# Bias tables of an attention layer: a stage of their own, or made in the first stage and copied in memory beside two feed-forward blocks

## The chip, the cores and the metric

The kernel runs on one core of a Trainium2 chip. The metric is the device time of one execution in microseconds (us). The core has a matrix engine (TensorE, PE in the profile), three engines for elementwise work (VectorE or DVE, ScalarE or ACT, GpSimd or POOL) and SyncE (SP), which issues transfers. Each engine runs its own instructions in order, and they meet at semaphores. Transfers run on 16 shared DMA engines.

## The reference

Eight blocks follow each other, each with a residual sum and a layer norm, on x of 4 x 1024 x 256 in f32: causal attention, two layers of local attention with a gated feed-forward each, attention with a relative position bias, a quantised projection, a state-space block, experts, a linear recurrence, and two more local layers. The change concerns the bias of the fourth block only (16 heads, no mask, 32 buckets):

```
line[h, r] = 4 * rel_emb[bucket(r - 1023), h]      # r = 0..2047
bias[h, q, k] = line[h, k - q + 1023]
out = softmax((Q K^T + bias) / 4) V                # /4 is applied inside the exponential
```

So all that a head needs is one line of 2048 numbers; each query row reads it one step further to the left.

## The kernel before

The program is a chain of some 30 stages. A stage opens its buffers and semaphores, runs a block with one instruction stream for each engine, and ends with a barrier of all engines; nothing of the next stage starts before it. Stages pass their data through DRAM.

`stage_enter` (lines 295 to 371) is the first. SP's queue copies the input in DRAM into the padded array `rows` (4 transfers of 1 MB, L315), writes 24 small strips of zeros (L319, L320), and then loads 32 tiles of the input (`enter_xin`, L326). PE turns each, ACT moves it out of PSUM and stores it as `cols` (L359). Beside them DVE and ACT make the tables of the recurrence (`RecurrenceTables`: DVE, then two sines on ACT after the first 8 tiles, then DVE).

`stage_gated_ffn` runs four times; B0ffn and B1ffn are the two in the layers ahead of the bias attention. GpSimd makes an identity and clears a small tile (L1760), and has nothing else to do in the stage. SP loads weights (`w1` at L1748) and activation rows (L1732, L188), PE does the products (L1834, L1853), ACT the gelu and the stores of the results.

`stage_bias_tables` stands after B1ffn and ahead of Cqkv, the first stage of the bias attention. PE multiplies the embedding by a one-hot table (L1443), DVE scales it by 4 (L1464), SP stores the 16 lines (L1421), waits, and loads two of their columns (`bias_sides`, L1424), from which GpSimd and DVE make the far constants `ext_s` (stored at L1434). Then a loop over 16 heads makes two tables each. SP loads 128 shifted copies of the line (L1431: row p begins p elements later), PE turns the order of the rows round with a flipped identity (L1452) and does the same along the columns for a narrow table (L1457), DVE and ACT move both out of PSUM, and ACT's queue stores `skewed` (960 KB a head) and `near_s` (192 KB a head). Catt reads all three.

```
src = line[bass.ds(it * 2 + s, 1), :]
sp.dma_start(rows[:, s, :], bass.AP(src.tensor, src.offset, [[1, P], [1, W]])).then_inc(rows_in[s], 16)
```

Of the kernel before, what the change touches and what calls it, by code (L numbers as in the profile page):

```python
# [16 lines left out]
ALU = mybir.AluOpType  # L17
# [8 lines left out]
P = 128  # L26
# [268 lines left out]
def stage_enter(nc, x, act0, acts, tables, logs):  # L295

    with ExitStack() as ctx:
        pl = Pool_(nc, ctx, "enter")
        tables.working(pl)
        xin = pl.sb("xin", [P, IN, C])  # L300
# [11 lines left out]
        def _(sp):  # L312
            tables.load(sp, logs)
            for b in range(B):
                sp.dma_start(act0["rows"][b * TP + PAD:(b + 1) * TP, :], x[b * T:(b + 1) * T, :]).then_inc(copied, 16)  # L315
            sp.wait_ge(zeroed, 1)
# [5 lines left out]
            with sp.Fori(0, B) as it:  # L322
                for u in range(NT):
                    sp.wait_ge(t_done, it * NT + (u + 1))
                    apart(sp, pl.sp_unread)
                    sp.dma_start(xin[:, u % IN, :], x[bass.ds(it * T + u * P, P), :]).then_inc(x_in[u % IN], 16)  # L326
            sp.wait_ge(pads, 16 * 2 * B * len(acts))
            sp.wait_ge(copied, 16 * B)

        @block.gpsimd  # L330
        def _(g):
            g.memset(zero[:], 0.0).then_inc(zeroed, 1)
            make_identity(nc, g, ident, made)

        @block.tensor
# [33 lines left out]
        @block.vector  # L369
        def _(v):  # L370
            tables.make(v)

# [555 lines left out]
def stage_thin_attention(nc, name, q_s, k_s, v_s, nm_s, r_s, oT_s, scale, bias=None):  # L928
# [5 lines left out]

    causal = bias is None
# [437 lines left out]
def stage_bias_tables(nc, rel_emb, onehot, line, skewed, near_s, ext_s):  # L1373

    nb, H = rel_emb.shape
    W = 2 * T - P
    cuts = [(c, min(c + 512, W)) for c in range(0, W, 512)]  # L1380
    NC, RING = len(cuts), 5
    with ExitStack() as ctx:
        pl = Pool_(nc, ctx, "bias")
        emb, hot, out = pl.sb("emb", [nb, H]), pl.sb("hot", [nb, 2 * T]), pl.sb("out", [H, 2 * T])
        flip = pl.sb("flip", [P, P])
        rows, win = pl.sb("rows", [P, 2, W]), pl.sb("win", [P, 2, W])
        near = pl.sb("near", [P, 2, 3 * P])
        far, rest, sides = pl.sb("far", [P, 2, NT]), pl.sb("far_rest", [P, NT]), pl.sb("sides", [P, 2])
        far_b = pl.sb("far_b", [P, PARTS, NT], BF16)
        ext = pl.sb("ext", [P, PARTS, NT, P], BF16)  # L1390
        ps = pl.ps("ps", (P, 2 * T))
        nr_ps = [pl.ps(f"near{i}") for i in range(2)]
        loaded, made, flipped, copied, stored = (pl.sem(n) for n in ("loaded", "made", "flipped", "copied", "stored"))
        rows_in = [pl.sem(f"rows_in{i}") for i in range(2)]
        turned, near_turned, win_done, near_done = (pl.sem(n) for n in ("turned", "near_turned", "win_done", "near_done"))
        sides_in, placed, ext_done, ext_out = (pl.sem(n) for n in ("sides_in", "placed", "ext_done", "ext_out"))
        win_out = [pl.sem(f"win_out{i}") for i in range(2)]
        block = ctx.enter_context(nc.Block())

        @block.gpsimd  # L1400
        def _(g):
            g.memset(flip[:], 0.0)
            g.drain()
            g.affine_select(out=flip[:], in_=flip[:], compare_op=ALU.not_equal, fill=1.0, base=-(P - 1),
                            pattern=[[1, P]], channel_multiplier=1).then_inc(flipped, 1)
            g.wait_ge(sides_in, 32)
            for i in range(2):
                g.tensor_copy(far[:, i, :], sides[:, i:i + 1].to_broadcast([P, NT]))
                g.drain()
            g.affine_select(out=far[:, 0, :], in_=far[:, 0, :], compare_op=ALU.is_ge, fill=0.0, base=-2 * H,  # L1410
                            pattern=[[-H, NT]], channel_multiplier=1)
            g.drain()
            g.affine_select(out=far[:, 1, :], in_=far[:, 1, :], compare_op=ALU.is_ge, fill=0.0, base=-H - 1,
                            pattern=[[H, NT]], channel_multiplier=-1).then_inc(placed, 1)

        @block.sync
        def _(sp):
            sp.dma_start(emb[:], rel_emb).then_inc(loaded, 16)
            sp.dma_start(hot[:], onehot).then_inc(loaded, 16)
            sp.wait_ge(copied, 1)  # L1420
            sp.dma_start(line, out[:]).then_inc(stored, 16)  # L1421
            sp.wait_ge(stored, 16)
            for i, col in enumerate((0, 2 * T - 1)):
                sp.dma_start(sides[:, i:i + 1], line[:, col:col + 1].unsqueeze(0).to_broadcast([NT, H, 1]),  # L1424
                             allow_slow_non_contiguous=True).then_inc(sides_in, 16)
            with sp.Fori(0, H // 2) as it:
                for s in range(2):
                    sp.wait_ge(near_turned, it * 2 + (s + 1))
                    apart(sp, pl.sp_unread)
                    src = line[bass.ds(it * 2 + s, 1), :]  # L1430
                    sp.dma_start(rows[:, s, :], bass.AP(src.tensor, src.offset, [[1, P], [1, W]])).then_inc(rows_in[s], 16)  # L1431
            sp.wait_ge(ext_done, 1)
            for k in range(PARTS):
                sp.dma_start(ext_s.rearrange("(h k u) c -> k u h c", k=PARTS, u=NT)[k],  # L1434
                             ext[:, k].rearrange("p u c -> p (u c)")).then_inc(ext_out, 16)
            sp.wait_ge(ext_out, 16 * PARTS)

        @block.tensor
        def _(t):
            t.sem_inc(near_turned, 2)  # L1440
            t.wait_ge(loaded, 32)
            for c in range(0, 2 * T, 512):
                ins = t.matmul(ps[0:H, c:c + 512], emb[:], hot[:, c:c + 512], start=True, stop=True)  # L1443
            ins.then_inc(made, 1)
            t.wait_ge(flipped, 1)
            t.wait_ge(copied, 1)
            with t.Fori(0, H // 2) as it:
                for s in range(2):
                    t.wait_ge(rows_in[s], it * 16 + 16)
                    t.wait_ge(win_done, it * 2 + (s + 1))  # L1450
                    for c, e in cuts:
                        ins = t.matmul(ps[:, c:e], flip[:], rows[:, s, c:e], start=True, stop=True)  # L1452
                    ins.then_inc(turned, 1)
                    t.wait_ge(near_done, it * 2 + (s + 1))
                    for k in range(3):
                        x = T - k * P
                        ins = t.matmul(nr_ps[s][:, k * P:(k + 1) * P], rows[:, s, x:x + P], flip[:], start=True, stop=True)  # L1457
                    ins.then_inc(near_turned, 1)
# [1629 lines left out]
```

## Time and profile before

| | |
|---|---|
| median of 3 runs | 7667.36 us (7658.31 to 7671.06) |
| the profiled execution | 7661.74 us, its span 7660.0 us |
| busy over the span | PE 84%, DVE 61%, ACT 36%, POOL 17% |
| mean granted TensorE clock | 0.92 |
| DMA queues, share of 16 engines | SP's 23.8%, ACT's 13.2%; POOL's none |

Busy shares are means over stages that differ. Since stages are separated by barriers, the span is the sum of the stages, and the length of a stage is read between the first instruction of it on SP's queue and that of the next.

### The profile page before, as it was taken

The numbers are of one execution on the slowest core, as the hardware profiler recorded it, in microseconds if no ns is written. First come the engines' busy times: TensorE is split into PE (matmuls) and PEld (weight loads), VectorE is DVE, ScalarE is ACT, GpSimd is POOL, SyncE is SP. The second block draws the span as 40 slices with busy tenths as digits, with TensorE's granted clock in tenths as the row PEclk, the third lists the DMA queues.
The fourth block names the chain that finished last, engine by engine and source line by source line (L and its number), as shares of the span: only waits on it lengthen the run. The fifth ranks groups of instructions, "written<-read, shape, count | busy, mean of one in ns | idle before, by whom it ended". The sixth has DMA issues, their size and how long they took to land. (4 is left out here: it accounts for less than half of the span.)

```text
span 7660.0 us, 115272 instructions
## 1 busy us (share of the span) xinstructions
PE 6397.9 (84%) x31876; PEld 3356.0 (44%) x31876; DVE 4648.5 (61%) x11517; ACT 2779.5 (36%) x6066; POOL 1304.2 (17%) x1035
## 2 busy tenths in 40 slices
PE   6788868989998966999994387986996888998979
PEld 2333334655555533333332253334554455544655
DVE  5665467733864634888875747984335765347735
ACT  0255514712462200566661104541110255224711
POOL 1101115100610003000000003550002441015100
PEclk9899979989999987999997599997998899999999
DMA  5423244542455255332323221115222355324541
GB/s 177 117 67 70 54 148 153 175 143 73 138 184 169 76 213 188 81 80 71 85 57 106 80 80 56 37 32 143 67 64 74 126 163 183 99 87 151 178 150 54
DMA packets 931136, 851.29 MB, mean 111 GB/s; under 512 B 222216, under 2 KB 785376, under 8 KB 930464
## 3 DMA queue, kind: packets, MB, share of 16 engines
q1 hardware_dynamic: 500624, 522.99, 23.8%
q10 hardware_dynamic: 430080, 323.08, 13.2%
q8 instruction: 206, 3.38, 0.2%
q14 instruction: 226, 1.85, 0.1%
HBM read 503.10 MB, written 346.00 MB: 111 GB/s over the span
## 5 line engine op out<-in xcount | busy, mean ns | idle before, releaser
L1267 ACT ACTIVATE Catt_E<-Catt_t 128x512 f32<-128x512 f32 x1024 | 582.5, 596 | 345.8 <-DVE Catt_t L1230 164.0
L1216 DVE CUSTOM_DVE_ANT_0 Catt_S<-Catt_s,Catt_win 128x1024 f32<-128x1024 f32 x512 | 622.7, 1218 | 90.7 <-PE Catt_s L1139 62.1
L1216 DVE CUSTOM_DVE_ANT_0 Aatt_S<-Aatt_s,Aatt_win 128x128 f32<-128x128 f32 (+7 forms) x512 | 375.6, 757 | 251.4 <-PE Aatt_s L1139 239.8
L1267 ACT ACTIVATE Aatt_E<-Aatt_t 128x512 f32<-128x512 f32 (+3 forms) x768 | 355.2, 489 | 250.2 <-PE Aatt_t L1171 171.5
L1168 PE MATMUL Catt_t<-Catt_Q,Catt_K 123*128 123x512 bf16 x1024 | 369.3, 385 | 38.4 <-ACT Catt_E L1267 17.4
L1139 PE MATMUL Catt_s<-Catt_K,Catt_Q 96*128 96x512 bf16 x1024 | 321.2, 397 | 22.2 <-DMA Catt_K<-k_parts 12.1
L1194 PE MATMUL Catt_o<-Catt_E,Catt_V 128*32 128x256 f32 x4096 | 326.5, 391 | 0.0
L2358 PE MATMUL scan_cum<-scan_X,scan_upto 128*128 128x512 f32 x512 | 265.3, 608 | 25.3 <-DVE scan_X L2427 23.9
L1168 PE MATMUL Aatt_t<-Aatt_Q,Aatt_K 99*128 99x512 bf16 (+3 forms) x768 | 241.4, 333 | 51.9 <-ACT Aatt_E L1267 27.6
L2356 PE MATMUL scan_cum<-scan_X,scan_after 128*128 128x512 f32 x448 | 239.7, 617 | 44.0 <-DVE scan_pi L2438 44.0
L1230 DVE TENSOR_TENSOR Catt_t<-Catt_t,Catt_near 128x384 f32<-128x384 f32 (+1 forms) x384 | 200.4, 522 | 116.6 <-PE Catt_t L1168 112.9
L1139 PE MATMUL Aatt_s<-Aatt_K,Aatt_Q 96*128 96x512 bf16 (+3 forms) x768 | 219.8, 342 | 34.3 <-DVE Aatt_nmax L1216 20.8
L1194 PE MATMUL Aatt_o<-Aatt_E,Aatt_V 128*32 128x256 f32 (+1 forms) x2816 | 218.1, 354 | 0.0
L1168 PEld LDWEIGHTS Catt_t<-Catt_Q,Catt_K 123*128 123x128 bf16 x1024 | 96.4, 97 | 277.2 <-ACT Catt_E L1267 222.0
L2625 ACT ACTIVATE moe_sg<-moe_g 128x512 f32<-128x512 f32 x80 | 47.8, 597 | 367.3 <-PE moe_u L2568 367.2
L2568 PE MATMUL moe_g<-moe_xc,moe_wg 128*128 128x512 f32 x320 | 160.4, 625 | 13.0 <-DVE moe_hid L2701 12.7
L2358 PEld LDWEIGHTS scan_cum<-scan_X,scan_upto 128*128 128x128 f32 x512 | 99.5, 196 | 155.0 <-issue 152.0
L1139 PEld LDWEIGHTS Catt_s<-Catt_K,Catt_Q 96*128 96x128 bf16 x1024 | 59.0, 98 | 243.7 <-DVE Catt_nmax L1216 138.9
L2339 POOL TENSOR_TENSOR scan_pr<-scan_pr,scan_pi 128x1024 f32<-128x1024 f32 x64 | 150.9, 2357 | 42.0 <-DVE scan_pr L2438 42.0
L2356 PEld LDWEIGHTS scan_cum<-scan_X,scan_after 128*128 128x128 f32 x448 | 83.3, 195 | 169.8 <-issue 153.7
L2144 PE MATMUL state_in_z<-state_in_wj,state_in_xc 128*128 128x288 f32 x512 | 142.6, 435 | 16.3 <-DVE state_in_wj L2169 16.3
L2332 POOL TENSOR_TENSOR scan_X<-scan_cs,scan_r 128x1024 f32<-128x1024 f32 x64 | 121.8, 1902 | 192.1 <-DVE scan_X L2427 192.1
(723 smaller groups left out, 14584.6 us busy)
## 6 DMA issues: line engine op xcount, KB each, us to landing
moe_cb<-c_s SPq DMA_DIRECT2D x16, 1024.0 KB
bias_rows<-line SPq DMA_DIRECT2D x16, 960.0 KB, 7.1
skewed<-bias_win ACTq DMA_DIRECT2D x16, 960.0 KB
Catt_win<-skewed SPq DMA_DIRECT2D x16, 960.0 KB, 5.0
rec<-state_in_r ACTq DMA_DIRECT2D x32, 416.0 KB
scan_r<-rec SPq DMA_DIRECT2D x64, 208.0 KB, 2.5
Aatt_Q<-q_parts SPq DMA_DIRECT2D x32, 384.0 KB, 4.4
Aatt_K<-k_parts SPq DMA_DIRECT2D x32, 384.0 KB, 5.6
```

The lines of the kernel that those rows point to most:

```text
L1139: ins = t.matmul(s_ps[j % 2][:, c:d], Q[0:K0, b, h, u * P:(u + 1) * P], K[0:K0, b, h, c:d], start=True, stop=True)
L1168: ins = t.matmul(t_ps[n % 2][:, 0:hi - lo], K[:, b, h, kb * P:(kb + 1) * P], Q[:, b, h, lo:hi], start=True, stop=not diagonal and n not in ...
L1194: ins = t.matmul(o_ps[f:f + 2 * hd, o + k0 * P:o + k1 * P], V[:, b, kb, h, :], blocks[:, h, x, k0:k1, :], start=kb == 0 and c == 0, stop=c ...
L1216: v.tensor_tensor_reduce(out=S[:, j % 2, 0:w], in0=s_ps[j % 2][:, 0:w], in1=win[:, 0 if causal else h, w0:w0 + w], scale=-1.0, scalar=BIG, ...
L1230: v.tensor_tensor(x, x, near[:, b, h, a - (kb - 1) * P:z - (kb - 1) * P], ALU.add).then_inc(near_done, 1)
L1267: a.activation(E[:, kb % NB, h, lo:hi], t_ps[n % 2][:, 0:hi - lo], ACT.Exp, scale=scale).then_inc(exped, 1)
L2144: t.matmul(z_ps[s][:], xc[:, c, kt, q * P + j + 1:q * P + j + 1 + P], wj[:, kt, j, :], start=j == 0 and kt == 0, stop=j == TAPS - 1 and kt ...
L2332: g.tensor_tensor(X[:, m % 4, 0, :].rearrange("p (k e) -> p k e", k=16), cs[:, m % 2, :].rearrange("p (k e) -> p k e", k=16), r[:, m % R, ...
L2339: g.tensor_tensor(pr[:, m % 2, :], pr[:, m % 2, :], pi[:, m % 2, :], ALU.add).then_inc(sum_done, 1)
L2356: t.matmul(cum[i][:, c:c + 512], after[:], X[:, (j - 1) % 4, i, c:c + 512], start=False, stop=False, skip_group_check=True)
L2358: ins = t.matmul(cum[i][:, c:c + 512], upto[:], X[:, j % 4, i, c:c + 512], start=u == 0, stop=True, skip_group_check=True)
L2568: ins = t.matmul(ps[k % 2][:], w[:, kt, j * P:(j + 1) * P], xc[:, c, kt, :], start=kt == 0, stop=kt == KT - 1)
```

## The change

The stage goes. A class `BiasTables` takes its parts:

- In `stage_enter`, SP loads the embedding and the one-hot table ahead of the four copies, and after these waits for the lines, stores them, waits for the store and loads the two columns, all ahead of the zero strips and the tile loop. PE makes the lines; it also turns the middle 512 columns of the lines (four transposes, four products with the flipped identity), so that a second short array `back` holds them in reverse order. DVE copies each result out ahead of the recurrence tables, and makes the far constants behind them. SP stores `back` and the far constants after its loop and waits for them.
- In B0ffn and B1ffn, GpSimd's queue issues for four pairs of heads each one copy from DRAM to DRAM for `skewed` and one for `near_s`: 256 rows of 7680 bytes and 256 of 1536 bytes, each row read one element further left than the one before. GpSimd then waits for all 8 before it can reach the barrier.

```diff
+    def store_lines(self, sp):
+        sp.wait_ge(self.copied, 1)
+        sp.dma_start(self.lines, self.out[:]).then_inc(self.stored, 16)
+        sp.wait_ge(self.stored, 16)
+        for i, col in enumerate((0, 2 * T - 1)):
+            sp.dma_start(self.sides[:, i:i + 1], self.lines[0:self.H, col:col + 1].unsqueeze(0).to_broadcast([NT, self.H, 1]),
+                         allow_slow_non_contiguous=True).then_inc(self.sides_in, 16)
...
+    def copy(self, v):
+        H = self.H
+        v.wait_ge(self.lined, 1)
+        v.tensor_scalar(self.out[:], self.ps[0:H, :], 4.0, None, ALU.mult).then_inc(self.copied, 1)
+        v.wait_ge(self.parts, 1)
+        v.tensor_copy(self.turned[:], self.ps[:, 0:4 * H].rearrange("p (k h) -> p k h", k=4)).then_inc(self.parts_copied, 1)
+        v.wait_ge(self.turned_back, 1)
+        v.tensor_copy(self.back_sb[:], self.ps[0:H, 512:512 + 4 * P]).then_inc(self.back_copied, 1)
...
+    def store(self, sp):
+        sp.wait_ge(self.back_copied, 1)
+        sp.dma_start(self.back, self.back_sb[:]).then_inc(self.ext_out, 16)
+        sp.wait_ge(self.ext_done, 1)
+        for k in range(PARTS):
+            sp.dma_start(self.ext_s.rearrange("(h k u) c -> k u h c", k=PARTS, u=NT)[k],
+                         self.ext[:, k].rearrange("p u c -> p (u c)")).then_inc(self.ext_out, 16)
+        sp.wait_ge(self.ext_out, 16 + 16 * PARTS)
+
+    def spread(self, g, pairs, out):
+
+        for i in pairs:
+            up, down = self.lines[i * 2:i * 2 + 2, P - 1:2 * T], self.back[i * 2:i * 2 + 2, P:4 * P]
+            for src, to, step, w in ((up, self.windows, 2 * T, 2 * T - P), (down, self.nears, 4 * P, 3 * P)):
+                g.dma_start(to.rearrange("(h p) c -> h p c", p=P)[i * 2:i * 2 + 2], bass.AP(src.tensor, src.offset, [[step, 2], [-1, P], [1, w]])
+                            ).then_inc(out, 16)
+        g.wait_ge(out, 32 * len(pairs))
...
             tables.load(sp, logs)
+            bias.load(sp)
             for b in range(B):
                 sp.dma_start(act0["rows"][b * TP + PAD:(b + 1) * TP, :], x[b * T:(b + 1) * T, :]).then_inc(copied, 16)
+            bias.store_lines(sp)
             sp.wait_ge(zeroed, 1)
...
+            bias.store(sp)
             sp.wait_ge(pads, 16 * 2 * B * len(acts))
...
             t.sem_inc(t_done, IN)
+            bias.product(t)
             t.wait_ge(made, 1)
+            bias.turn(t, ident)
...
         def _(v):
+            bias.copy(v)
             tables.make(v)
+            bias.split(v)
...
-def stage_bias_tables(nc, rel_emb, onehot, line, skewed, near_s, ext_s):
...
             g.memset(wl_sb[:], 0.0).then_inc(wl_zero, 1)
+            if aside:
+                bias, pairs = aside
+                bias.spread(g, pairs, spread_out)
...
-    stage_bias_tables(nc, i["L1_attn_rel_emb"], i["onehot"], line, skewed, near_s, ext_s)
```

## Rows read from the trace of the kernel before

**Rows 1.** Timeline of SP's queue, the bias stage and the first of Cqkv

```profile
2734.11 0.34 SPq L1418 DMA_DIRECT2D bias_emb<-in_L_attn_rel_emb  x1
2734.50 0.54 SPq L1419 DMA_DIRECT2D bias_hot<-in_onehot  x1
2747.15 0.33 SPq L1421 DMA_DIRECT2D line<-bias_out  x1
2749.70 1.41 SPq L1424 DMA_DIRECT2D bias_sides<-line  x2
...
2843.59 3.35 SPq L1434 DMA_DIRECT2D ext_s<-bias_ext  x3
2864.07 0.41 SPq L493 DMA_DIRECT2D Cqkv_w_q<-in_L_wq  x1
```

**Rows 2.** Timeline of PE and DVE, first part of the bias stage

```profile
2737.80 7.00 PE L1443 MATMUL bias_ps<-bias_hot,bias_emb 32*16 32x512 f32 x8 [9.15 <-DMA bias_hot<-in_onehot]
2744.84 2.28 DVE L1464 TENSOR_SCALAR bias_out<-bias_ps 16x2048 f32<-16x2048 f32 x1 [18.61 <-PE bias_ps L1443]
2755.67 1.90 DVE L1477 COPY bias_ext<-bias_far_b 128x1024 bf16<-128x1024 bf16 x3
```

**Rows 3.** Timeline of SP's queue, first 21 us: copies, strips, tiles

```profile
1.27 2.66 SPq L315 DMA_DIRECT2D rows<-in_L_attn_x  x4
3.97 0.55 SPq L319 DMA_DIRECT2D rows<-enter_zero  x1
...
16.02 0.39 SPq L320 DMA_DIRECT2D cols<-enter_zero  x1
...
19.34 0.38 SPq L320 DMA_DIRECT2D cols<-enter_zero  x1
20.19 1.11 SPq L326 DMA_DIRECT2D enter_xin<-in_L_attn_x  x2
```

**Rows 4.** Timeline of the first stage: recurrence tables, and the next stage's start

```profile
15.05 0.15 DVE L2784 TENSOR_SCALAR enter_cr<-enter_aw 128x1 f32<-128x1 f32 x1
...
31.48 1.28 ACT L2759 ACT_TABLE_LOAD   x1 [0.44 <-ACT enter_xt L357]
...
49.84 0.75 DVE L2807 SCALAR_TENSOR_TENSOR rec_rot<-rec_rot,enter_st,enter_tt 128x512 f32<-128x512 f32 x1
...
63.01 0.40 SPq L493 DMA_DIRECT2D Aqkv_w_q<-in_wq  x1
```

**Rows 5.** Busy time by stretch: B0ffn and B1ffn behind GpSimd's clearing

```profile
1612.00:1898.00 286.00, 268.05 (x864) 148.21 (x864) 110.51 (x336) 68.79 (x145) 0.07 (x1) 0.96 0.23 67
2438.00:2731.00 293.00, 268.03 (x864) 148.22 (x864) 162.97 (x528) 68.80 (x145) 0.32 (x2) 0.95 0.27 79
```

The columns are the stretch and its length, busy us (and instructions) of PE, weight loads, DVE, ACT, POOL, the granted clock, the busy share of the 16 DMA engines, and GB/s.

**Rows 6.** Timeline, start of B0ffn

```profile
1611.76 0.31 POOL L1760 MEMSET B0ffn_wl<- 128x256 f32 x1
...
1616.89 0.39 SPq L1748 DMA_DIRECT2D B0ffn_w<-in_L_ffn_w  x1
...
1624.82 3.75 PE L1834 MATMUL B0ffn_g<-B0ffn_hT,B0ffn_w 128*128 128x512 f32 x4 [0.94 <-issue]
```

**Rows 7.** Transfers issued, whole run: KB each, median us to landing

```profile
bias_rows<-line SPq DMA_DIRECT2D x16, 960.0 KB, 7.1
...
Catt_win<-skewed SPq DMA_DIRECT2D x16, 960.0 KB, 5.0
...
v_s<-B0qkv_vo ACTq DMA_DIRECT2D x32, 256.0 KB, 2.1
...
B0ffn_w<-in_L_ffn_w SPq DMA_DIRECT2D x1, 1364.0 KB, 5.8
```

**Rows 8.** DMA queues in the first 21 us: packets, MB, share of 16 engines

```profile
q1 hardware_dynamic: 3632, 4.30, 68.8%
```

**Rows 9.** Timeline in Catt: a 256 KB transfer with four source rows, and its reader

```profile
3148.18 0.59 ACTq L1296 DMA_DIRECT2D Catt_Rb<-r_s  x1
3153.04 1.27 POOL L1122 TENSOR_TENSOR Catt_O<-Catt_O,Catt_Rb 128x512 f32<-128x512 f32 x1 [16.95 <-DMA Catt_Rb<-r_s]
```

More of the change, by code:

```diff
@@ L297, in stage_enter @@
+def stage_enter(nc, x, act0, acts, tables, logs, bias):
     with ExitStack() as ctx:
@@ L299, in stage_enter @@
         tables.working(pl)
+        bias.working(pl)
         xin = pl.sb("xin", [P, IN, C])
@@ L333, in _ @@
             make_identity(nc, g, ident, made)
+            bias.flip(g)
+            bias.place(g)
         @block.tensor
@@ L1710, in stage_gated_ffn @@
         hid_done = pl.sem("hid_done")
+        spread_out = pl.sem("spread_out")
         block = ctx.enter_context(nc.Block())
@@ L2953, in bass_post_layernorm_stack, with local_transformer @@
     nm_s = nc.dram_tensor("nm_s", [8 * B, 2 * PARTS * T], BF16, kind="Internal").ap()
-    def local_transformer(name, pre, x, final=None):
+    def local_transformer(name, pre, x, final=None, bias=None):
         h = a2
@@ L2965, in local_transformer @@
             stage_gated_ffn(nc, f"{name}{l}ffn", h, g("ln_gc"), g("ln_bc"), g("w1"), g("b1c"), g("w2"), g("b2"), y,
-                            base=x if l else None, final=final if l else None)
+                            base=x if l else None, final=final if l else None,
+                            aside=(bias, range(l * 4, l * 4 + 4)) if bias else None)
             src = y
@@ L2971, in bass_post_layernorm_stack @@
     tables = RecurrenceTables(nc, kept)
-    stage_enter(nc, i["L0_attn_x"], a0, acts, tables, i["L3_logs"])
+    lines, back, skewed, near_s = scratch("lines", [16, 2 * T]), scratch("back", [16, 4 * P]), scratch("skewed", [16 * P, 2 * T - P]), scratch("near_s", [16 * P, 3 * P])
+    ext_s = nc.dram_tensor("ext_s", [16 * PARTS * NT, T], BF16, kind="Internal").ap()
+    bias = BiasTables(i["L1_attn_rel_emb"], i["onehot"], lines, back, skewed, near_s, ext_s)
+    stage_enter(nc, i["L0_attn_x"], a0, acts, tables, i["L3_logs"], bias)
     cur = a0
@@ L2978, in bass_post_layernorm_stack @@
     cur = a1
-    cur = local_transformer("B", "L0_ffn", cur)
-    line, skewed, near_s = scratch("line", [16, 2 * T]), scratch("skewed", [16 * P, 2 * T - P]), scratch("near_s", [16 * P, 3 * P])
-    ext_s = nc.dram_tensor("ext_s", [16 * PARTS * NT, T], BF16, kind="Internal").ap()
-    stage_bias_tables(nc, i["L1_attn_rel_emb"], i["onehot"], line, skewed, near_s, ext_s)
+    cur = local_transformer("B", "L0_ffn", cur, bias=bias)
     nxt = a1 if cur is a0 else a0
```

189 lines of the change are left out of this document (69 added, 120 removed).

## The prediction

> **What bounds the kernel now.** I read the timeline of SP's queue first, since stages stand behind each other with barriers between: a stage is worth the distance between its first transfer and that of the next. For the bias stage this is 2864.07 - 2734.11 = 129.96 us [rows 1]. Nothing of a neighbour lies in this stretch, so all of it is on the path. Then I read the stages that take the work over. In B0ffn and B1ffn PE is busy 268 of 286 and 268 of 293 us, while the 16 DMA engines are busy 23% and 27% and POOL does nothing behind its clearing [rows 5]: PE sets these stages, and the copies have idle queues beside them. In the first stage SP's queue comes first: its first tile load is issued at 20.19, and until then it handles four copies and 24 strips [rows 3]. PE and ACT cannot start a tile before that, so what is put ahead of the tile loads on SP's queue delays the stage.
>
> **Removed.** The whole stage, with its barrier: -129.96 us. The stage that follows now begins where the bias stage began. B1ffn's last stores had to land before either.
>
> **Moved into the first stage, SP's queue.** Where the first copy is issued now, at 1.27 [rows 3], stands the load of the embedding, and the one-hot table follows 0.39 later as in [rows 1], at 1.66. From there I use the distances of the bias stage. PE starts 3.30 us after the one-hot table is issued (2737.80 - 2734.50): 4.96. DVE starts 7.04 us behind that (2744.84 - 2737.80): 12.00. SP issues the store 2.31 later: 14.31. It passes its wait for the landing 2.55 later (2749.70 - 2747.15): 16.86. The two column loads take 1.41 to issue: 18.3 [rows 1, 2]. The four input copies are issued in the meantime and lie under this wait, as SP is not held by them. Then the 24 strips: at the end of the old sequence 8 of them took 19.34 - 16.02 = 3.32, 0.415 each; the last is issued 23 x 0.415 = 9.5 behind the first, at 27.8, and the first tile 0.85 later, at 28.7. Against 20.19 that is +8.5 us. Old strips took 15.37 us for the same 23 steps (3.97 to 19.34), because SP was held up while the copies ran; part of the new wait takes the place of that. Bounds: if PE's eight products run in half the 7 us, +5.0; if the strips are held as before, 15.37 instead of 9.5, +14.4. I take +8.5, since by 18 us the copies are through.
>
> **The rest of the first stage, at nothing.** PE's transposes and products for `back` (8 small ones) and DVE's two copies fall between 14.3 and about 19, when no tile has landed. DVE starts the recurrence tables about 17 us later, so its hand-over to ACT moves from 15.2 to about 32; ACT asks for it after 8 tiles, at 31.48 now and 40.0 then [rows 4], so 8 us of cover are left. If that cover were gone, ACT would hold up its own tile loop, one for one. The far constants are queued behind DVE's last table step, which ends at 50.6 and then at 59.1; a few steps and the 1.90 us of copies [rows 2] bring it to about 62.5. SP's loop ends later than that, and its four stores at the end (3.35 us for three of them [rows 1], plus some 2.5 to land, the distance of the line's store) come to about 70, while the stage ends near 63.0 + 8.5 = 71.5 [rows 4]. That is 1.5 us of cover; if it fails, the bill is a few us, and it lies inside the +14.4.
>
> **Moved into B0ffn and B1ffn.** POOL is free at 1612.1 [rows 6] and the barrier comes at about 1898: 286 us, and 293 in the other stage [rows 5]. A stage copies 4 pairs x (1920 + 384) KB = 9216 KB, 9.44 MB. No copy with such rows exists in the trace. The nearest is the input's: 4.30 MB kept SP's queue on 68.8% of 16 engines for 21 us, 231 engine-us, so one engine copies 18.6 KB in a us [rows 8]. That makes 9440/18.6 = 507 engine-us, or 32 us if spread over all 16. That the source is shifted by 4 bytes a row costs nothing visible: the bias stage loads such rows at 960 KB in 7.1 us beside stores of equal volume, against 5.0 for aligned ones without such company [rows 7]. Over how few engines a copy can go while it stays hidden: 286 us less what the stage's own traffic takes of each engine, 0.23 x 286 = 66, leaves 220, so 507/220 = 2.3 engines. (The far smaller 1536-byte rows may be dearer, but are a sixth of the volume.)
>
> The pair of heads is the outermost step of each copy, and it counts two. A transfer whose source has four outer rows, 256 KB, took 4.86 us from issue to its reader, where 256 KB from 128 partitions land in 2.1 [rows 9, 7]: an outer count under 16 seems to narrow a transfer. With two engines for each copy, the longest takes 1966/(2 x 18.6) = 53 us, and four pairs of heads take 53 to 254 us, according to whether they go side by side on different engines or all on the same two. The Trainium skill (DMA: Bandwidth & Descriptors, "Why a DMA increments its semaphore by 16 and not by 1") says that a transfer uses the largest number of engines up to 16 that divides the outermost count of both sides, here 2, and that GpSimd's transfers take their engines by a cursor that goes round. By that rule the eight copies of a stage would share out all 16 engines and the stage's copies would take about 53 us; the trace agrees as far as the four-row transfer shows. A cursor that stood still is the second rival.
>
> What the copies cost the stage while they run: weights `w1` are issued at 1616.89, land 5.8 us later at 1622.7, and PE's first product stands at 1624.82 [rows 6, 7], 2.1 later. Company stretches a load by 7.1/5.0 = 1.4 [rows 7]: to 8.2 us, landing at 1625.1, about on time; the first activation rows, on the path, lose about 1 us in the same way, and the small last weights are queued behind `w1`. I take +2 us a stage. Bounds: nothing, if the copies' first descriptors come late; +6 a stage if the loads of the start take double. Later loads are issued a whole chunk of four tiles ahead of their use, and PE's 268 of 286 us [rows 5] leave them little to hold up. Sum of both: +4 (0 to +12). GpSimd's issuing costs no engine anything: it has no other work there.
>
> **Sum.** -130.0 + 8.5 + 4.0 = -117.5 us. Against the profiled execution's 7661.74 this gives 7544; the median of the runs is 5.6 above that execution, so I forecast a median of 7550. The bounds of the parts give -130 + 5 = -125 to -130 + 14.4 + 12 = -103.6, that is 7542 to 7564.
>
> **The rivals.**
>
> First, the copies go on the same two engines and are not hidden. 507/2 = 254 us, plus the stage's own traffic on these engines, 66 and 0.27 x 293 = 79: 320 and 333 us against 286 and 293. Both barriers come late, by 34 and 40 us: -117.5 + 74 = -43.5, 7624. For it speaks the outer count of two; against it that a queue which holds several transfers would leave 14 engines idle. A slower descriptor writer than SP's would look alike: to be late it must take over 286/2048 rows = 0.14 us a row.
>
> Second, the other side: a copy runs on one engine, or at half the rate on two. Then a stage's copies take 507 + 66 = 573 us, 287 beyond B0ffn's end, and 293 beyond B1ffn's: -117.5 + 580, 8130, slower than before. It decides from an overrun of 59 us a stage, copies of 345 us; that is a combined rate under 9440/279 = 34 KB/us. Nothing in the trace shows GpSimd's queue at all, so it cannot be excluded; against it stands that even two engines of the measured rate reach 37.
>
> Third, the first stage grows by more than counted: the strips are held, the line's store waits behind 1 MB copies in the same queue, the recurrence tables come late. With +20 instead of +8.5 the time is 7562, still well ahead; there is no room here for more than half of the 130.
>
> **How the numbers follow.** Hidden copies 0.72 (7550, own range 7542 to 7564). Same two engines or slow descriptors, an overrun between 0 and 74 us, 0.14 (7624 at its full size). One engine or half the rate 0.07 (8130). A larger first stage 0.07 (7562). The range takes the first and the last case, half of the second, and 7 us of the spread between runs at the lower end: 7535 to 7600, which leaves out 0.07 and 0.07, and the tails. A measurement of this kernel can tell a change from none at about 0.2%, 15 us. Faster: all but the second rival and a rest, 0.91; within 0.2%: 0.02; slower: 0.07.
>
> **What would show it.** The first tile load on SP's queue near 28.7, and the next stage's first transfer near 71.5. ACT's sines with no new wait in front. In B0ffn and B1ffn the distance from the stage's first transfer to that of the next longer than before by about 2 us, with the DMA share raised in their first 50 to 100 us and falling back. PE at 268 us busy in both. Cqkv's first transfer where the bias stage began. The prediction is wrong if POOL is the engine that ends a feed-forward stage, waiting for the landing of its copies, or if the DMA share stays raised to the barrier; and wrong in size if the first stage moves by other than 5 to 15 us.

## The result and the profile after

The changed kernel takes 7639.41 us (median of 12 runs, 7635.93 to 7653.48); the kernel before takes 7667.88 beside it (12 runs). The ratio is 0.9963, with an interval of 0.9955 to 0.9971. It is faster, by 28 us. I had forecast 117.5 us less, at 7550, with a range of 7535 to 7600. The sign came out, and the size did not.

The profiled execution took 7639.54 us with a span of 7637.8; that of before took 7661.74 and 7660.0. So 22.2 us have to be explained, against the 117.5 of the sum. The first reading is again the timeline of SyncE's queue, since its first transfer of each stage says where the time went. The first rows belong to the first stage of the changed kernel, and answer to [rows 3, 4]:

```profile
1.73 0.42 SPq L319 DMA_DIRECT2D enter_hot<-in_onehot  x1
2.19 3.21 SPq L434 DMA_DIRECT2D rows<-in_L_attn_x  x4
14.54 0.32 SPq L358 DMA_DIRECT2D lines<-enter_out  x1
18.56 1.40 SPq L361 DMA_DIRECT2D enter_sides<-lines  x2
...
30.83 34.79 SPq L446 DMA_DIRECT2D enter_xin<-in_L_attn_x  x32
65.83 0.34 SPq L395 DMA_DIRECT2D back<-enter_back  x1
66.22 2.42 SPq L398 DMA_DIRECT2D ext_s<-enter_ext  x3
77.34 0.41 SPq L620 DMA_DIRECT2D Aqkv_w_q<-in_wq  x1
```

The first tile load is at 30.83 instead of the forecast 28.7, and the next stage begins at 77.34 instead of 71.5. One can see the wait for the lines (5.40 to 14.54) and the wait for their landing (14.86 to 18.56) in the gaps of the queue.

B0ffn of the changed kernel, same view, answers to [rows 6]. These are SyncE's and GpSimd's queues:

```profile
1629.19 3.78 SPq L1731 DMA_DIRECT2D B0ffn_hs<-rows  x8
...
1637.66 1.49 SPq L1747 DMA_DIRECT2D B0ffn_w<-in_L_ffn_w  x1
1639.20 3.29 SPq L1750 DMA_DIRECT2D B0ffn_wl<-in_L_ffn_w  x2
...
1649.79 15.02 SPq L1753 DMA_DIRECT2D B0ffn_w<-in_L_ffn_w  x1
1665.24 12.54 SPq L1731 DMA_DIRECT2D B0ffn_hs<-rows  x8
```

```profile
1630.15 1.22 POOL L407 DMA_DIRECT2D skewed<-lines  x1 [0.16 <-issue]
...
1636.62 1.10 POOL L407 DMA_DIRECT2D skewed<-lines  x1
1687.66 1.07 POOL L407 DMA_DIRECT2D near_s<-back  x1 [49.94 <-issue]
```

And PE and DVE in the same stretch:

```profile
1639.88 0.43 DVE L1773 BATCH_NORM_STATS2 B0ffn_st<-B0ffn_hs 128x6 f32<-128x256 f32 x1 [7.04 <-DMA B0ffn_hs<-rows]
1645.73 0.43 DVE L1773 BATCH_NORM_STATS2 B0ffn_st<-B0ffn_hs 128x6 f32<-128x256 f32 x1 [5.42 <-DMA B0ffn_hs<-rows]
...
1650.41 1.11 PE L1823 MATMUL B0ffn_h<-B0ffn_ident,B0ffn_hn 128*128 128x128 f32 x4 [25.85 <-DVE B0ffn_hn L1784]
...
1673.20 3.78 PE L1837 MATMUL B0ffn_g<-B0ffn_hT,B0ffn_w 128*128 128x512 f32 x4 [16.06 <-DMA B0ffn_wl<-in_L_ffn_w]
```

PE's first product with the weights stands 44.0 us behind the first transfer of the stage (1673.20 - 1629.19). Before it was 13.6 (1624.82 [rows 6] against 1611.27). The kernel before, for comparison:

```profile
1611.27 3.68 SPq L1732 DMA_DIRECT2D B0ffn_hs<-rows  x8
```

```profile
1620.76 1.11 PE L1820 MATMUL B0ffn_h<-B0ffn_ident,B0ffn_hn 128*128 128x128 f32 x4 [14.13 <-DVE B0ffn_hn L1781]
```

First the activation rows are late: PE turns the first tile (L1823) 21.2 us into the stage instead of 9.5, which is 11.7 of the 30.4 us. Then it waits for the two small last pieces of the weights, `wl`. The view of transfers by stretch, 1629 to 1690, shows how late:

```profile
q0 software_dynamic: 10593, 9.11, 46.7%
q1 hardware_dynamic: 5040, 3.90, 21.5%
...
B0ffn_w<-in_L_ffn_w SPq DMA_DIRECT2D x1, 1364.0 KB, 12.2
B0ffn_hs<-rows SPq DMA_DIRECT2D x16, 64.0 KB, 5.3
...
B0ffn_wl<-in_L_ffn_w SPq DMA_DIRECT2D x2, 42.0 KB, 25.8
```

q0 is GpSimd's queue and q1 SyncE's; the columns are packets, MB and the share of 16 engines. The 1364 KB of weights land in 12.2 us where they took 5.8 [rows 7]. A load of 42 KB takes 25.8, where it took 5.7. So it is not the large load that suffers most. The busy time by stretch shows that PE did nothing up to 1650, half of the next 50 us, and then worked without a gap (the columns are those of [rows 5]):

```profile
1629.00:1650.00 21.00, 0.00 (x0) 0.00 (x0) 4.13 (x21) 0.00 (x0) 8.31 (x10) 0.52 0.79 229
1650.00:1700.00 50.00, 24.95 (x56) 11.01 (x57) 9.46 (x32) 8.74 (x18) 1.07 (x1) 0.69 0.58 183
1700.00:1800.00 100.00, 98.86 (x328) 55.24 (x326) 41.19 (x126) 25.73 (x55) 0.00 (x0) 1.00 0.22 63
```

Last, the end of the program. DVE stands still twice in the last feed-forward block, H1ffn, where it did not before; here it is the first time, with PE behind it:

```profile
7427.74 1.41 DVE L1794 SCALAR_TENSOR_TENSOR H1ffn_hid<-H1ffn_a,H1ffn_b,H1ffn_gl 128x512 f32<-128x512 f32 x2 [6.53 <-issue]
```

```profile
7428.54 2.07 PE L1837 MATMUL H1ffn_g<-H1ffn_hT,H1ffn_w 128*128 128x512 f32 x2 [6.92 <-DVE H1ffn_hid L1794]
```

Worked out in this way for all kernels of this text, from profiled executions (stage lengths from first transfer to first transfer, H1ffn from its first transfer to the end of the span; "product" is the distance from B0ffn's first transfer to PE's first product with its weights; all in us):

| kernel | first stage | B0ffn | B1ffn | H1ffn | all else | span | product |
|---|---|---|---|---|---|---|---|
| before | 63.0 | 288.9 | 296.6 | 289.8 | 6591.7, and 130.0 bias | 7660.0 | 13.6 |
| after | 77.3 | 324.8 | 329.2 | 305.2 | 6601.3 | 7637.8 | 44.0 |
| e1_late | 78.1 | 293.7 | 302.9 | 304.5 | 6589.1 | 7568.3 | 13.9 |
| e2_small | 77.4 | 327.0 | 331.5 | 305.5 | 6596.8 | 7638.2 | 45.5 |
| e4_half | 77.6 | 322.4 | 327.1 | 304.9 | 6592.8 | 7624.8 | 45.6 |
| e5_shift | 80.1 | 294.1 | 303.1 | 291.3 | 6605.9 | 7574.5 | 13.7 |
| e6_quarters | 76.9 | 302.2 | 308.9 | 305.4 | 6605.3 | 7598.7 | 25.6 |
| e7_enter | 70.3 | 297.6 | 299.4 | 306.5 | 6595.8 | 7569.6 | 14.0 |
| e8_best | 70.7 | 292.4 | 298.4 | 290.0 | 6606.4 | 7557.9 | 13.6 |
| e9_eight | 77.8 | 349.1 | 355.2 | 304.3 | 6597.4 | 7683.8 | 52.3 |
| e10_both | 70.7 | 293.9 | 299.7 | 290.4 | 6598.2 | 7552.9 | 13.7 |
| e11_drains | 77.5 | 324.9 | 331.0 | 290.8 | 6595.4 | 7619.6 | 44.3 |
| e12_many | 78.5 | 329.6 | 334.0 | 304.8 | 6603.9 | 7650.8 | 53.4 |
| e13_wide | 79.0 | 324.2 | 331.0 | 304.3 | 6595.2 | 7633.7 | 47.5 |

"All else" runs from 6589 to 6606 from one profile to another, without order. So a total tells two kernels apart only beyond some 15 us, but each stage is good for 2 to 3. From before to after: -130.0 + 14.3 + 35.9 + 32.6 + 15.4 = -31.8, and +9.6 in the rest: -22.2.

### The profile page after: what moved, and what is told of

Same layout as the page of the kernel before. It is cut to its first block and busy times, and to the rows that moved or that the text cites. A ratio compares the mean times of both kernels' runs of the same rounds, so it can differ in the third digit from the quotient of the medians.

```text
span 7637.8 us, 114466 instructions
## 1 busy us (share of the span) xinstructions
PE 6340.9 (83%) x31664; PEld 3321.1 (43%) x31664; DVE 4615.5 (60%) x11503; ACT 2780.8 (36%) x6050; POOL 1321.7 (17%) x1051
## 3 DMA queue, kind: packets, MB, share of 16 engines
q0 software_dynamic: 22144, 18.99, 0.8%
```

## The experiments

My theory after this profile: the copies at the start of B0ffn and B1ffn delay the stage's own loads. The rivals were the volume of the copies, code placement, and something that has nothing to do with when the copies go.

**e1_late: the copies start when the first half of the first batch is through.**

```diff
             if aside:
                 bias, pairs = aside
+                g.wait_ge(tail.y_done, NT + 4)
                 bias.spread(g, pairs, spread_out)
```

> The changed kernel with one wait more: GpSimd issues its copies only after the first four tiles of the stage have been multiplied out, so that no copy stands beside the loads of the stage's start. Theory (the copies hold up the first loads: B0ffn and B1ffn are 36 and 33 us longer, all of it before PE's first product): both stages return to 289 and 297 us within 5, and the time falls by 60 to 69 to about 7575. Rival (copies beside the stage cost what their volume takes, wherever they are put): both stages stay 25 to 36 us longer, time about 7640.

7574.07 us (4 runs, 7569.97 to 7588.57), ratio to before 0.9886 (0.9869 to 0.9902). The same 9.4 MB go from 49 us in instead of 1 us, and the product comes at its old place:

```profile
1645.38 3.74 PE L1838 MATMUL B0ffn_g<-B0ffn_hT,B0ffn_w 128*128 128x512 f32 x4 [0.94 <-issue]
```

B0ffn falls from 324.8 to 293.7 and B1ffn from 329.2 to 302.9. So the position of the copies in the stage costs 57 us in the two stages together; their mere company, later in the stage, costs 4.8 and 6.3.

**e5_shift: e1_late, and the code of all later stages of DVE lies 26 instructions further on.**

```diff
             bias.split(v)
+            for _ in range(26):
+                v.drain()
```

> As the first kernel of this call, with 26 instructions that do nothing on DVE at the end of the first stage, by which DVE's program is as long again as that of the kernel before. The changed kernel's last stage is 15 us longer than before, with two stalls of 6.5 us on DVE that no semaphore explains, and instruction transfers beside them. Theory (the place of DVE's loop in its program decides whether each turn of it has to be fetched again): the two stalls are gone and H1ffn takes 286 us to its last stores, as before, not 301; time 12 to 15 us under the first kernel's. Rival (the stalls are chance, or come from elsewhere): they stay, or are gone in both.

7571.10 us (7565.93 to 7578.69), ratio 0.9874 (0.9858 to 0.9891). Both stops of DVE in H1ffn are gone, and H1ffn is 291.3 instead of 304.5. Nothing in this stage was edited. I had expected 12 to 15 us less in all. The median moved by 3 only, which the spread of the runs swallows; I come back to it at e11_drains.

**e2_small: each row of 7680 bytes written as four pieces in one access pattern.**

```diff
-                g.dma_start(to.rearrange("(h p) c -> h p c", p=P)[i * 2:i * 2 + 2], bass.AP(src.tensor, src.offset, [[step, 2], [-1, P], [1, w]])
+                n = 4 if w > 3 * P else 1
+                g.dma_start(to.rearrange("(h p) (j c) -> h p j c", p=P, j=n)[i * 2:i * 2 + 2],
+                            bass.AP(src.tensor, src.offset, [[step, 2], [-1, P], [w // n, n], [1, w // n]])
```

> The changed kernel with each row of 7680 bytes cut into four pieces of 1920 bytes, same volume, same start. Theory of turns (each small piece of a load waits for one whole piece of a copy on engines that take turns between queues): a turn falls from 291 ns to about 84, so the delay of PE's first product in B0ffn (44 us behind the stage's first instruction, 14 before) shrinks from 30 to 10 or 15 us. Rival (the copies' volume occupies the engines until they are through): the delay stays at 27 to 33 us.

One run: 7639.94 us. In the stretch of B0ffn's first 61 us GpSimd's queue moved 9.09 MB in 10368 packets, where the changed kernel's moved 9.11 in 10593; over the whole run both moved 18.99 MB in 22144. The edit did not change the packets, so it tells nothing about their size.

**e4_half: two pairs of heads at the start, two late.**

```diff
-                bias.spread(g, pairs, spread_out)
+                bias.spread(g, pairs[0:2], spread_out)
+                g.wait_ge(tail.y_done, NT + 12)
+                bias.spread(g, pairs[2:4], spread_out, 64)
```

> The changed kernel with two of the four pairs of heads copied at the stage's start, and two only after twelve tiles. Half the volume at the start, on fewer engines, but as long on each. Theory of turns: a load that is spread over all 16 engines lands with the slowest of them, so the delay of PE's first product stays at 20 us or more of 30. Rival (volume): it falls to half, 15 us or less.

One run: 7626.56 us. The product comes 45.6 us in, as late as with all copies. Half the volume takes nothing off the delay, so it isn't the volume in total, and so hardly the memory's bandwidth. The view of transfers, 1660 to 1668, shows what is going on while `wl` is awaited:

```profile
DMA packets 176, 0.85 MB, mean 106 GB/s; under 512 B 59, under 2 KB 59, under 8 KB 176
...
q0 software_dynamic: 89, 0.68, 20.2%
q1 hardware_dynamic: 87, 0.16, 5.2%
```

A quarter of the engines' time is in use, and still a 42 KB load isn't through. The two queues move 89 and 87 packets: one for one. The 89 of q0 are rows of 7680 bytes (0.68 MB / 89 = 7.6 KB) and take 0.202 x 16 x 8 = 25.9 engine-us, 0.29 each. The 87 of q1 are for the most part (59) under 512 bytes. Both queues together use 25.4% of 16 engines, the time of 4.1; I read this as four engines that work without a gap, two for each of the two long copies, and twelve that have nothing to do. So on an engine that copies, a packet of the load goes after a row of the copy, then the next, whatever its own size. The order is inferred from these counts, since the view doesn't tell engines apart. And it holds for this stretch only: in the changed kernel's first 8 us of copies (1630 to 1638) q0 moved 3834 packets with 0.51 MB, 133 bytes in the mean, so what held the activation rows there is not taken apart. Half the pairs keep half as many engines, but each of them as long, and a load that is spread over 16 engines is done when its slowest part is.

**e6_quarters: each copy as four, of a quarter of the columns.**

```diff
+                q = w // 4
+                for c in range(0, w, q):
-                g.dma_start(to...[i * 2:i * 2 + 2], ... [[step, 2], [-1, P], [1, w]])
+                    g.dma_start(to...[i * 2:i * 2 + 2, :, c:c + q], ... [[step, 2], [-1, P], [1, q]])
```

> As the changed kernel, with the window copies still at the start of the two feed-forward blocks, but each copy is cut into four column ranges, so that a row that is read and written is 1920 bytes long (384 for the short tables) instead of 7680 (1536), with the same bytes and four times as many rows. Turns (each packet of a block's own loads waits for one row of the copies on a shared engine, so what counts is how long one row holds an engine): a row takes about a quarter of 0.3 us plus its fixed part, so the first product of the gate and up weights, 44 us into the stage in the changed kernel and 13.6 before, comes at 18 to 28 us, and each of the two stages is 12 to 25 us shorter than the changed kernel's 325 and 329: 7590 to 7615 in all. Volume (the copies' bytes fill the engines or the memory until they are through): the same bytes, so 40 us or more into the stage as before, stages of 322 or longer, and 7635 or more; if the short rows are dear for the engines, then later still.

One run: 7600.40 us, product at 25.6, within what turns predicted. But the reason was not sound. GpSimd issues seven copies at once and then stands before the eighth, here for 21.1 us:

```profile
1642.30 3.20 POOL L409 DMA_DIRECT2D near_s<-back  x3
1666.58 1.07 POOL L409 DMA_DIRECT2D near_s<-back  x1 [21.09 <-issue]
```

So with pieces a quarter as large there was also a quarter as much in flight while the loads came. And the rows did not become 1920 bytes: in the stretch 1646 to 1654 q0 moved

```profile
q0 software_dynamic: 765, 1.54, 65.1%
```

which is 2013 bytes a packet in the mean, more than a whole quarter row; rows were joined.

**e9_eight: a quarter of the columns, but of all eight heads; eight copies as before.**

```diff
-        for i in pairs:
+        for k in range(4):
-                g.dma_start(to...[i * 2:i * 2 + 2], ... [[step, 2], [-1, P], [1, w]])
+                g.dma_start(to...[h0:h1, :, k * q:k * q + q], ... [[step, h1 - h0], [-1, P], [1, q]])
```

> As the changed kernel, copies at the start of the blocks, but each copy now takes one quarter of the columns of all eight heads instead of all columns of two heads. So as many copies as before (eight, seven of them in flight at once) with the same bytes are under way when the block's own loads come, and only the row is short, 1920 bytes. In the kernel with quarters of two heads each, fewer bytes were in flight (seven pieces of at most 480 KB), so its early first product (25.6 us into the block, 44 in the changed kernel) may be owed to the row's length or to the smaller amount. Row length (turns): a turn of about 0.13 us instead of 0.3 again, a first product 24 to 32 us in, the stages 300 to 310, 7600 to 7615 in all. Amount in flight: the copies now lie on all 16 engines for over 30 us, the first product comes 40 us in or later, the stages stay at 322 or more, and the time at 7630 or more.

One run: 7685.50 us, slower than the changed kernel and than the kernel before. The product comes 52.3 us in, and B0ffn is 349.1. The eighth copy waits longer:

```profile
1717.45 1.07 POOL L409 DMA_DIRECT2D near_s<-back  x1 [74.78 <-issue]
```

So e6's gain came, by this comparison of single runs, from the smaller amount in flight and not from shorter rows. That falsifies what I read out of e6. It doesn't refute turns: here too rows were joined (1.04 MB in 280 packets in one stretch of 8 us, 3.7 KB each), and the queue held its eighth copy for 75 us. The delay goes with the time for which copies lie queued, as far as GpSimd's wait before its eighth transfer measures it: this wait is 21, 50 and 75 us in e6_quarters, the changed kernel and e9_eight, and the product comes at 25.6, 44.0 and 52.3; e4_half has copies of the size of the changed kernel's, and 45.6. I had no case of rows that were really short.

**e12_many and e13_wide: one more load, which nobody uses, ahead of the weights in every feed-forward block.**

```diff
             w1_k = w1.rearrange("(k p) n -> p k n", p=P)
+            sp.dma_start(more[:], w1[0:P, 0:16:2])      # e12_many: 1024 packets of 4 bytes
+            sp.dma_start(more[:], w1[0:P, 0:1024])      # e13_wide: 128 packets of 4096 bytes
```

> The changed kernel, and in each of the four feed-forward blocks one more load by SyncE's queue, ahead of the gate and up weights, which nobody uses: 128 partitions of 8 elements that do not lie side by side, so 1024 packets of 4 bytes, 4 KB in all, some 64 for each of the 16 engines. The two last blocks have no copies beside them and show what the load costs by itself. Turns (on an engine that copies, each packet of a load waits for one row of a copy, 0.29 us, however small it is): 64 turns are 18.6 us on top in the two blocks with copies, first product about 60 us in instead of 44, each of them 12 to 20 us longer than 325 and 329, and only 0 to 4 us in the last two: 7665 to 7680 in all. Volume or a shared bandwidth: 4 KB is nothing, so the blocks with copies grow no more than the last two, by 0 to 4 us each: 7640 to 7656.

> As the kernel with the load of 1024 small packets, but the unused load is 128 partitions of 1024 elements side by side: 512 KB, in 128 packets of 4096 bytes, 8 for each engine. Turns: 8 turns of 0.29 us and the 8 packets' own time, 3 to 6 us more in the blocks with copies, 1 to 4 in the two without: 7645 to 7660 in all, less than with the 1024 small packets although it moves 128 times the bytes. Volume or a shared bandwidth: 512 KB beside copies that take half the engines' time costs far more than 4 KB, 5 to 15 us in each block with copies, and more than the small packets cost there.

One run each: 7652.50 and 7635.37 us. PE's first products, e12_many in B0ffn and in H0ffn (no copies there), then e13_wide in B0ffn:

```profile
1688.38 3.78 PE L1840 MATMUL B0ffn_g<-B0ffn_hT,B0ffn_w 128*128 128x512 f32 x4 [24.19 <-DMA B0ffn_wl<-in_L_ffn_w]
...
6528.97 3.75 PE L1840 MATMUL H0ffn_g<-H0ffn_hT,H0ffn_w 128*128 128x512 f32 x4 [0.95 <-DMA H0ffn_wl<-in_L_ffn_w]
```

```profile
1679.39 3.78 PE L1840 MATMUL B0ffn_g<-B0ffn_hT,B0ffn_w 128*128 128x512 f32 x4 [18.88 <-DMA B0ffn_wl<-in_L_ffn_w]
```

Beside copies, 4 KB in 1024 packets move the product from 44.0 to 53.4, and 512 KB in 128 packets move it to 47.5. Without copies, in H0ffn, either leaves it at 13.7 (6528.97 - 6515.32, and 6512.60 - 6498.9). So what a load pays beside copies is paid for each packet and not for bytes: the order that turns predict and that a shared bandwidth reverses. The size is half of what I expected: 9.4 us for 64 packets an engine are 0.15 each, not 0.29; and of 9.4 only 4.8 reach the end of each of the two stages, where I had expected 12 to 20. The totals don't speak for turns: 7652.5 lies in the rival's range, and e13_wide comes out under its own. A later product is given back in part within the stage, and the differences of these single runs are within the 15 us named above.

**e7_enter: e1_late, with the lines stored and the edge columns fetched by GpSimd's queue.**

```diff
         def _(sp):
             ...
-            bias.store_lines(sp)
             sp.wait_ge(zeroed, 1)
         def _(g):
             ...
             bias.flip(g)
+            bias.store_lines(g)
             bias.place(g)
```

> The kernel with the copies late (7574.1 in its run, first stage 78 us in its profile against 63.0 in the kernel before), with one more edit: the lines are stored, and the two edge columns fetched, from GpSimd's queue instead of SyncE's, so SyncE goes on to the zero strips and the tile loads at once. If the first stage is longer because SyncE stands in front of its loads while the lines are made, the first tile load comes at 20 to 22 us instead of 30.8, the last column tile is stored by 63, and what ends the stage is then VectorE's last part (its rotary values end at 61.3, the strips of the far table at 65, 2.4 us of issues and some 4 us to land): a stage of 70 to 73 us, 5 to 8 shorter, and 7566 to 7569 in all. Rival: the stage is bound by its transfers as a whole (DMA share 0.9 and more); then the loads start early and spread, the last column tile is stored after 70, the stage stays at 76 to 78 and the time at 7574.

7571.94 us (4 runs, 7566.09 to 7575.19), ratio 0.9874 (0.9857 to 0.9890). The first stage is 70.3 instead of 78.1:

```profile
9.26 5.37 SPq L438 DMA_DIRECT2D rows<-enter_zero  x1
...
23.27 34.66 SPq L445 DMA_DIRECT2D enter_xin<-in_L_attn_x  x32
...
70.35 0.42 SPq L620 DMA_DIRECT2D Aqkv_w_q<-in_wq  x1
```

The first load comes 7.6 us earlier, later than I expected by 1.3, because now the strips are held while the copies run (5.37 us for one). So the wait of SyncE was the cost for the larger part. Of the 7.3 us over the 63.0 of before that remain, 3.1 lie ahead of the first tile load (23.27 against 20.19), and 4.2 behind it, where the stores at the end meet the last column tiles. The total moved by less than the spread of the runs.

**e8_best: e7_enter and the 26 drains.**

> As the kernel before this one in the list (copies late, lines stored from GpSimd's queue), with 26 drains behind VectorE's last work of the first stage, which set the code of all later stages 26 instructions further on. In the last feed-forward block VectorE stands still for 6.5 us twice, at the turn of the loop, in every run without this shift, and in none with it, and that block was 298.9 us long without and 284.4 with it. If that stall is lost time, 7555 (7550 to 7562); if, as the two kernels' medians in the earlier runs say (7574.1 and 7571.1), other stages give most of it back, 7563 to 7567.

7561.32 us (4 runs, 7556.76 to 7570.96), ratio 0.9864 (0.9847 to 0.9880). H1ffn is 290.0 instead of 306.5. The time is within the range of my first case (7550 to 7562) and 2 us short of the second, so it doesn't decide between them.

**e10_both: e8_best, and the quarters of e6_quarters.**

> The fastest kernel so far (copies late, lines stored from GpSimd's queue, drains; 7561.3, two feed-forward blocks of about 292 and some 3 to 5 longer than in the kernel before) with the copies also cut into column quarters of 1920 bytes. Turns: the loads of the running block's own batches wait less, 2 to 4 us less a block, 7554 to 7560. Rival: in the running part nothing waits for those loads, so 7561 stays as it is; or the four times as many packets hold the engines longer (about 14.8 KB a us for each engine instead of 19.4) and cost up to 5 us, 7566.

7555.24 us (4 runs, 7546.89 to 7567.34), ratio 0.9860 (0.9843 to 0.9876). B0ffn and B1ffn are 293.9 and 299.7 against 292.4 and 298.4: no less, so the rival was right that nothing waits for loads there. The intervals of e8_best and e10_both overlap, and I don't call one faster. Both beat the changed kernel by about 1%, and before by 1.4%.

**e11_drains: the changed kernel and the 26 drains alone.**

> The changed kernel with nothing but the 26 drains behind VectorE's last work of the first stage. If the two stops of 6.5 us of VectorE in the last feed-forward block hang on where its code lies, they are gone here as in the two other kernels with this shift, and that block goes from 300 to about 285 us. If that is worth its whole length, 7625; if as much as the two pairs of medians so far (3.0 and 10.6 us), 7629 to 7637; if the stops have nothing to do with the code's place, 7639 and both stops still there.

7626.48 us (4 runs, 7621.27 to 7632.10), ratio 0.9953 (0.9937 to 0.9970). DVE in H1ffn, at the turn of the loop where the changed kernel stood for 6.53 us:

```profile
7419.19 1.41 DVE L1796 SCALAR_TENSOR_TENSOR H1ffn_hid<-H1ffn_a,H1ffn_b,H1ffn_gl 128x512 f32<-128x512 f32 x2 [0.72 <-issue]
```

H1ffn is 290.8. Over the 14 profiles it is 289.8 to 291.3 in before and in the four kernels with the drains, and 304.3 to 306.5 in the nine without. That DVE's stops hang on where the code lies is shown; that the total gains the whole 14.5 is not. The three pairs of medians differ by 3.0, 10.6 and 12.9 us, the last from two sets of runs, and the intervals of the ratios overlap in each pair.

## Why the prediction was wrong

**Removed, -130.0: right.** Cqkv's first transfer follows B1ffn, and nothing of the stage is left on the path.

**The first stage, +8.5 (5 to 14.4): +14.3.** Mis-sized. The chain up to the store was right (14.54 against 14.31), and the eight products took their 7.00 us again. The landing took 4.0 us instead of the 2.55 that I took from the bias stage: 1.5. That the 1 MB copies in the same queue are the cause isn't shown: from GpSimd's queue the same store took 6.3 us (e7_enter, 14.65 to 20.95). Strips were 0.43 each and not 0.415: 0.4. At the end, "1.5 us of cover" was not there: SyncE's loop ended at 65.6, and the three stores of the far constants ran into ACT's last column tiles, so the stage took 46.5 us from its first tile load, where it had taken 42.8: 3.7. This last reading is from the timeline; no run tests it. The third rival named the late landing of the lines' store; it is 1.5 of the 5.8 us.

**ACT's sines: right.** They came at 42.34 with 0.44 us of idle time before them, as before [rows 4].

**The copies, hidden: right.** 53 us by two engines of 18.6 KB a us was the estimate for the longest copy. GpSimd's queue began between 1632 and 1634; it used 44.0% of 16 engines in 1678 to 1686 and 12.2% in 1686 to 1694, so the four long copies took about 54 us. It moved 18.99 MB in the whole run in 0.8% of 16 x 7637.8 engine-us, which is some 19.4 KB a us (18 to 21 by the rounded share). The copies went side by side and did not end any stage; the first and second rivals fall. In 1662 to 1670, when only rows of the long copies moved (200 packets, 1.54 MB), the queue used 45.5% of 16 engines, 7.3 for four copies. This agrees with the rule of the Trainium skill (DMA: Bandwidth & Descriptors, "Why a DMA increments its semaphore by 16 and not by 1") on the number of engines that the prediction named, two for each copy.

**The step that failed is "What the copies cost the stage while they run": +2 a stage (0 to +6), and it was +35.9 and +32.6.** I priced company by bytes: a load beside stores of equal volume took 1.4 times as long. The activation rows were to lose 1 us and cost 11.7 at PE's first turn of a tile; the small last weights, which I named as queued behind `w1`, had no price at all, and they are what PE's first product then waited for, to 30.4 us later than before. The row with the 1.4 came from loads beside stores on their way at full width. Here the company was rows of 7680 bytes, and many packets of the waiting loads had 168 or 512 bytes (42 KB / 256 for `wl`, 64 KB / 128 for the activation rows). e1_late shows that starting later removes 57 of the 68.5 us. e4_half shows that the volume doesn't set the delay. The one-for-one count and the pair e12_many and e13_wide show that what pays is packets and not bytes. By the count, each packet of a load meets one row, 0.29 us; by the pair of added loads, 0.15. So that a load pays for each packet beside copies is shown; that the engines take turns is what the counts say, and the exact rate is open. The Trainium skill (DMA: Bandwidth & Descriptors, "Queues, rings and completion order") says that each engine goes round the queues that have work for it, packet by packet, and calls a packet 9 to 17 descriptors as a rule. The counts agree with the going round, and not more: turns of one packet each, or of equal numbers on both sides, give the same counts. I read that page for the number of engines and did not price this rule; it would have given the small loads of the stage's start as the ones in danger, since PE's first product waits for them.

What remains of the two stages with the copies late, 4.8 and 6.3, is at the upper bound, +6, that I had put down for the whole.

**Not in the prediction at all: H1ffn, +15.4.** A stage that the change doesn't touch. By my count, which no row here shows, the change makes DVE's compiled program 26 instructions shorter, so that what comes behind the edit lies elsewhere; DVE then stands 6.5 us at each of two turns of a loop. The view of transfers of the 12 us around the first stop has, for the queue that brings instructions, first the changed kernel and then e11_drains in the same place:

```profile
q14 instruction: 4, 0.03, 0.9%
```

```profile
q14 instruction: 1, 0.01, 0.3%
```

Four packets instead of one. The Trainium skill (Runtime: NRT & Kernel Launch, "Instruction fetch mechanics") says that an engine holds two blocks of its program and that a jump out of them waits for a fetch; the runs agree with such a wait, and would give it 6.5 us. The place of the code as the cause is shown by the drains; the fetch as its mechanism rests on these two counts.

**The forecast's form.** Of my three other cases the third (a larger first stage) happened beside two costs that no case held. The time lies 39 us above the range, 7535 to 7600, which took in the sum of the bounds and half of the first rival. From -117.5 to -22.2 there are 95.3 us: 5.8 of the first stage, 68.5 - 4.0 of the copies' company, 15.4 of H1ffn, and the 9.6 in all the rest, which are within what one profile differs from another. The parts worked out too low all pointed one way.

## What to carry to other kernels

A background copy that is hidden at a stage's end can still cost at its start: see which loads the first product waits for, count their packets rather than their bytes, and let large-row copies begin behind that product. A single semaphore wait was worth about 60 us here (57 in the two stages, 61 by the ratios), twice what the change gave without it. Having less in flight at a time brought the first product forward as well; moving less in total, with each long copy under way as long, did not.

After any edit, compare also the stages that it doesn't touch. In a kernel with loops, code that became shorter can lose in another stage what it saved; a few drains ahead of the loops show whether that is so.

## What the runs showed of the hardware

- GpSimd stood before its eighth issue of a stage: 49.94 us in the changed kernel, 74.78 in e9_eight. In e6_quarters it issued seven at once, and seven more behind the wait. It isn't a limit on what is under way: in e4_half only three copies were, since the first four had long landed, and the eighth was held all the same:

```profile
1782.53 1.06 POOL L407 DMA_DIRECT2D skewed<-lines  x1
1830.07 1.06 POOL L407 DMA_DIRECT2D near_s<-back  x1 [46.48 <-issue]
```

  Nor did a short copy that was through let it go: in the changed kernel only rows of the long ones moved from 1662 on, and the eighth was issued at 1687.66. What lets it go isn't shown beyond that. An issue by GpSimd took 1.07 us, where SyncE's takes 0.3 to 0.5; beside the copies SyncE's issues were held as well, the one at 1649.79 for 15.02 us.
- A row of 7680 bytes from DRAM to DRAM took an engine 0.29 us while the packets of another queue went between (e4_half, 1660 to 1668).
- Access patterns on paper don't give the packets: four pieces of a row were joined again (e2_small, the same 22144 packets), and 1920-byte rows came as packets of 2.0 to 3.7 KB in the mean (e6_quarters, e9_eight). The 1024 rows of 7680 and 1024 of 1536 bytes of a stage came with some 11000 packets, more than half of them under 512 bytes.
- PE's granted clock in B0ffn of the changed kernel was 0.52 in the 21 us in which it did nothing (near the lower level, 1.2 GHz), 0.69 in the next 50 us, in which it was idle for half, and 1.00 (2.4 GHz) from 1700 on. A part of the first chunk therefore ran at the lower level: PE's first four products took 3.78 us, later ones 1.88; before it was the same, 3.75 [rows 6].
